# Mixture-of-experts stage of a two-layer transformer: scatters issued ahead of the gathers on GpSimd's queue

## What is computed

```python
x = x + _L0_attn_ref(_layernorm(x), w, w_out)             # linear attention, 16 heads
x = x + _L0_ffn_ref(_layernorm(x), router_w, w1, b1, w2, b2)   # the experts
x = x + _L1_attn_ref(_layernorm(x), w_attn, w_proj)       # causal attention, one key/value head
x = x + _L1_ffn_ref(_layernorm(x), wf_re, wf_im, bias)    # a filter in frequency space
```

## Time and profile before

| what | value |
|---|---|
| median of 3 runs | 752.31 us (749.36 to 752.98) |
| the profiled execution, its own time | 752.71 us |
| its span, first to last instruction | 751.0 us |
| TensorE busy | 618.1 us (82%), 4111 matmuls |
| VectorE busy | 521.4 us (69%) |
| ScalarE busy | 374.9 us (50%) |
| GpSimd busy | 391.2 us (52%) |
| 64 gathers (line 1045), POOL busy | 62.6 us, 978 ns each |
| 56 scatters (line 1036), POOL busy | 89.4 us, 1597 ns each |
| mean granted TensorE clock | 0.956 |

### The profile page before, as it was taken

How to read it: one execution, slowest core, us unless ns; L and a number is a source line. 1 busy time by engine, 2 the same in 40 slices (tenths; PEclk the granted TensorE clock), 3 DMA queues, 4 the chain that set the end, 5 groups by cost and what they waited for, 6 DMA issues and landing times.

```text
span 751.0 us, 14209 instructions
## 1 busy us (share of the span) xinstructions
PE 618.1 (82%) x4111; PEld 369.9 (49%) x4111; DVE 521.4 (69%) x1779; ACT 374.9 (50%) x800; POOL 391.2 (52%) x529
## 2 busy tenths in 40 slices
PE   2478888888405999999799778999999999999894
PEld 1235555554302688776566533545454545444453
DVE  8458888887794112225478859898989898987554
ACT  0322333331450423326622357777777777767873
POOL 0077777776004777776887554343434343433341
PEclk9989999999855999999999989999999999999997
DMA  9400000000040122244663244040304030200011
GB/s 297 133 0 1 1 0 0 0 1 0 16 140 28 49 43 39 39 93 84 110 98 35 26 82 53 10 59 10 59 10 60 9 60 9 60 5 2 24 52 42
DMA packets 45145, 34.55 MB, mean 46 GB/s; under 512 B 4304, under 2 KB 41728, under 8 KB 45072
## 3 DMA queue, kind: packets, MB, share of 16 engines
q1 hardware_dynamic: 33584, 25.15, 14.5%
q0 software_dynamic: 10144, 7.90, 7.5%
q10 hardware_dynamic: 1344, 0.62, 0.3%
HBM read 14.13 MB, written 9.70 MB: 32 GB/s over the span
## 4 chain that ended last, share of the span: by engine, by line
PE 46%; DVE 16%; issue 8%; ACT 4%; POOL 1%; DMA 1%; DVEq 0%; ACTq 0%; POOLq 0%
PE bank L2146 8%; PE wide L1275 6%; DVE masked L1744 6%; PE wide L2133 5%; PE wide L2082 5%; PE wide L1283 4%; PE bank L1283 4%; PE bank L2082 2%; PE wide L2158 2%; ACT L282 1%; DVE mx L1744 1%; DVE slot_t L886 1%; POOL x_row L1045 1%; PE bank L2057 1%; PE bank L1300 1%
## 5 line engine op out<-in xcount | busy, mean ns | idle before, releaser
L1941 ACT ACTIVATE pexp<-wide 128x512 f32<-128x512 f32 (+2 forms) x384 | 180.9, 536 | 77.9 <-PE wide L2133 75.9
L1744 DVE CUSTOM_DVE_ANT_0 masked<-wide,mask_qk 128x128 f32<-128x128 f32 (+3 forms) x423 | 182.8, 477 | 46.9 <-PE wide L2082 46.1
L1872 POOL TENSOR_SCALAR_AFFINE_SELECT pexp<-pexp 128x256 f32<-128x256 f32 x256 | 106.4, 429 | 166.7 <-ACT pexp L1941 165.2
L2133 PE MATMUL wide<-qT,kTe 128*128 128x256 bf16 (+3 forms) x512 | 121.8, 301 | 6.1 <-ACT pexp L1941 3.7
L2082 PE MATMUL wide<-kTm,qT 128*128 128x128 bf16 (+3 forms) x423 | 102.6, 300 | 13.2 <-DVE mx L1744 10.8
L1036 POOL DMA_INDIRECT x_dram<-yg,row_u x56 | 89.4, 1597 | 30.6 <-DVE yg L1088 15.7
L1225 ACT ACTIVATE hT<-wide,b1T 128x512 f32<-128x512 f32 x64 | 43.9, 686 | 100.7 <-PE wide L1275 100.7
L1045 POOL DMA_INDIRECT x_row<-xln_dram,row_u x64 | 62.6, 978 | 52.5 <-DVE slot_tok L915 33.6
L2146 PE MATMUL bank<-pexp,vx 128*32 128x512 f32 (+3 forms) x1024 | 85.4, 446 | 4.9 <-POOL pexp L1872 4.9
L2133 PEld LDWEIGHTS wide<-qT,kTe 128*128 128x128 bf16 x512 | 48.6, 99 | 42.5 <-ACT pexp L1941 23.1
L1275 PE MATMUL wide<-xgT,w_sb 128*128 128x512 f32 x128 | 67.4, 612 | 1.5 <-ACT xgT L1218 1.5
(11 more groups left out here) (282 smaller groups left out, 1046.6 us busy)
## 6 DMA issues: line engine op xcount, KB each, us to landing
qT<-qp SPq DMA_DIRECT2D x126, 64.0 KB
x_sb<-in_L_attn_x SPq DMA_DIRECT2D x8, 256.0 KB, 6.7
w_sb<-in_L_ffn_w SPq DMA_DIRECT2D x1, 2048.0 KB, 13.1
xln_dram<-hT SPq DMA_DIRECT2D x8, 256.0 KB, 2.3
x_dram<-x_sb SPq DMA_DIRECT2D x7, 256.0 KB, 2.7
x_sb<-x_dram SPq DMA_DIRECT2D x7, 256.0 KB, 3.1
out_x<-x_sb SPq DMA_DIRECT2D x7, 256.0 KB, 2.3
qT<-qp_first SPq DMA_DIRECT2D x18, 64.0 KB
```

The costliest lines, as they stand in the source:

```text
L1744: ins = nc.vector.tensor_tensor_reduce(out=masked[:, n % 4, at], in0=bank_of(n)[:, at], in1=mask_qk[:, T - w:T], scale=1.0, scalar=LEAST, ...
L1872: nc.gpsimd.affine_select(out=pexp[:, at, :, 0:P], in_=pexp[:, at, :, 0:P], pattern=[[0, 2], [1, P]], compare_op=ALU.is_ge, fill=0.0, base ...
L1941: nc.scalar.activation(pexp[:, exp_slot(b, 2 * step + h // 2), h % 2:h % 2 + nh, 0:w], scores_bank(b, m)[:, 0:nh * w].rearrange("p (h t) - ...
L2133: ins = nc.tensor.matmul(scores_bank(b, m)[:, hh * w:(hh + 1) * w], kTe[:, par, j * P:(j + 1) * P], qT[:, b % QB, 4 * qd + h + hh, j * P:T ...
```

## The change

In `moe_pool`, the gathers for the phase four further on are issued ahead of the wait for `m_y` in phases 0 to 3 only. In phases 4 to 11 they are issued behind that wait and behind the scatters of the phase, and ahead of the two small copies.

```diff
+        SCATTERS_LEAD = 4
+
         def moe_pool(pool):
...
             for p in range(PHASES):
-                if p + 4 < PHASES:
+                if p < SCATTERS_LEAD:
                     pool_moe_gathers(pool, p + 4)
                 pool.wait_ge(m_y, p + 1)
                 if p == E:
                     pool.wait_ge(m_xw[1], 16 * len(DMA_SECOND))
                 for b in half_of(p):
                     if b in BY_DMA:
                         pool_moe_scatter(pool, p % E, b)
+                if SCATTERS_LEAD <= p < PHASES - 4:
+                    pool_moe_gathers(pool, p + 4)
                 if p == E + 1:
                     pool_v(pool, 0, 0)
                 if p == E + 2:
```

## The result

The changed kernel takes 770.83 us (median; the kernel before, run beside it, 752.55). The ratio is 1.0251, with a 95% interval of 1.0216 to 1.0286: slower by some 18 us. One of its four executions took 3373.09 us, counts as a slow one and stands outside the ratio; the other three took 770.58 to 770.84. The same file, measured a second time further down, took 774.52 us, ratio 1.0277 (1.0255 to 1.0299).

The account below looks back on a forecast made before the run. TensorE, busy in all 44 us from 305 to 349 us, was taken as the bound, later POOL's round. Delays reaching 7.6, 13.7, 15.4 and 19.1 us on 752.7 made 771.8, less 0.4: 771.4 us, range 763 to 779.

Parts of the forecast that it names:

- Step 1: Transposes of phase 8: their gathers, now behind the scatters of phase 4, land late and stop TensorE for 4.6 us.
- Step 2: Behind the stop at phase 8: the granted clock falls, costing 3.0 us, so TensorE is 7.6 us late.
- Step 3: Transposes of phases 9 and 10: both gather blocks land in time, the second by 0.4 us, so no stop.
- Step 4: Transposes of phase 11: stop of 4.7 us, 1.6 beside another wait; clock falls again, 3.0; TensorE 13.7 us late.
- Step 5: Second half: POOL's round becomes the bound, with stops of 2.2 us at phase 13 and 4.3 at 15; TensorE 19.1 late.
- (b): Rival: it costs more, through slower landings beside the query rows or a third stop with its clock; 774 to 779, chance 0.12.
- The gain: Scatters no longer behind the next gathers: only the next scatter ever waited for one, 0.6 us in all; costed at nothing.
- The cost of a later S7: Scatters of phase 7: SP's loads of the first half's rows wait for them; said to move only as VectorE's output does.
- The signs: Marks expected in the trace, among them 15 to 20 us of gather waits and no POOL gaps over 2.5 us late on.
- (a): Rival: the clock doesn't fall behind the stops, 14.1 us late, 766.4; one fall of the two some 769; chance 0.20.
- (c): Rival: no difference, the gathers are in time all the same; 752.3 us, chance 0.03.
- (d): Rival: faster, as query rows land sooner and TensorE's 1.59 us stop ahead of the first maxima goes; 750.7, chance 0.03.

Follow-up runs that it names:

- the experiment with the wait alone: Against the kernel before: in phases 4 to 11 the gathers move behind the wait for VectorE's output but stay ahead of the scatters; 757.11 us, ratio 1.0055.
- The filled kernel: The changed kernel with 5, 5, 3 and 6 extra matmuls ahead of TensorE's wait for the gathers of phases 8, 11, 12 and 14; 770.22 us, ratio 1.0247.

## Why the prediction was right, point by point

The predicted 771.4 us stand against 770.83 and 774.52 measured, with a range of 763 to 779. The first agreement is closer than the working deserves, and that is luck: the stage was mis-sized by 2.5 and 3.4 us (19.1 for 21.6 and 22.5), and in the first measurement a front that was shorter by chance took that back. With the front of the kernel before, 752.3 and the measured stage make 774 to 775.

- **Step 1, right.** The stop at phase 8 is 4.53 us for a predicted 4.6. Alone, with its clock, it makes 6.6 us of the final time.
- **Step 2, right.** The clock's 3.0 us were 3.3 in the first profile and 4.2 in the second (y6 with and without the stop filled), and 2.7 with phase 4 alone. The mean over the 8 us behind the stop was 0.57, as predicted, and 0.50 in the second profile.
- **Step 3, right.** No stop at phases 9 and 10, and moving phase 6 alone costs nothing.
- **Step 4, right.** 4.56 us for 4.7, the clock at 0.63 over 8 us, and y9 late by 13.2 and 14.4 for 13.7.
- **Step 5, right in kind, wrong in its phases and too small.** "POOL's round becomes the bound" holds: with the rows held back the stage is still 21.8 us longer. But I followed the odd blocks, G13 (stop 2.2) and G15 (4.3), and the kernel stops at the even ones, G12 (3.16) and G14 (5.86). The sum had no landing for G12 and G14 at all, and for the block beside the query rows I took 3.0 us, while the last gather of G14 had 6.7 us to its reader. The transposes for phases 12 and 14 were in the trace before:

```profile
360.32 0.60 PE L1267 MATMUL wide<-cst,x_row 128*128 128x128 f32 x4
...
386.97 0.60 PE L1267 MATMUL wide<-cst,x_row 128*128 128x128 f32 x4
```

With the terms of step 5, S8 starts at 349.2 + 10.8 = 360.0, the last gather of G12 at 371.9, and with 2.5 us it lands at 374.4, wanted at 360.32 + 13.7 = 374.0. There was no slack, so any slower landing had to stop TensorE there. What I had in the rivals (b) as a risk on the last rounds was in the main line. The total was off by less, because a stop at phase 14 takes the place of the one at phase 15. With the query rows held back for both blocks the kernel comes near to what I wrote: a stop of 4.05 at phase 15, y12 late by 16.6 and y13 by 21.8 (15.4 and 19.1).
- **The gain, nothing, right as far as tested.** Where the order was changed and no gather came late (phase 6 alone), the time is that of the kernel before, and the scatters of the changed kernel still wait for one another for 0.6 us in all. The run with five buffers does not bear on this, since its queue is the old one.
- **The cost of a later S7.** The prediction said only that S7 moves as y7 does, which was true in the changed kernel. That a few us more would be paid in full was not seen; the experiment with the wait alone showed it, 5.7 us for 5.
- **The signs.** S12 starts 20.2 us later than before, counted from y4 (predicted 19). Two signs were missed a little: TensorE waits 22.8 us for gathers in all (21.0 in the second profile), not 15 to 20, and POOL has a gap of 2.69 us ahead of S10, not under 2.5.
- **Rivals.** (a), a clock that doesn't fall, is refuted by both profiles. The filled kernel, which keeps the clock up over the first two stops only, has 19.6 us in the stage and not the 14.1 of (a). (c) and (d) needed a lead of 12 us; phases 8 and 11 have 7.4 and 7.3, and both stopped.

What is not settled: why the second profile of the changed kernel is 0.8 us longer from y4 to y15 than the first, with the same stops within 0.8 us. Its clock was at 0.50 over the 8 us from 318.5 us, behind the first stop, where the first profile has 0.57; that fits, but no run isolates it. Nor does any run show what the new order does to the landings in the second half, where the query rows are under way as well.

## What to carry to other kernels

For each transfer in an engine's queue compare two times: from the moment that releases its issue, over all that stands ahead of it in the queue, to its landing; and from that same moment to the reader. Here the first was 12.0 us for 7.4 to 12.4 us of the second, and whether moving a block cost 6.6 us or nothing hung on that alone. Put what is read soonest first in the queue; a wait may stand ahead of it if the lead allows, a run of long issues may not. And write the queue out in full before comparing two loops: the one with its scatters first and its gathers five phases ahead looks like the change, but gives the old queue and the old time.

## What the runs showed of the hardware

The last gather of a block comes 4 to 5 us later beside 18 SyncE transfers of 64 KB than without them (6.7 us from issue to reader in the changed kernel, 7.8 us to landing with the rows held for phase 14, against 2.5), and holding these back moves the delay to the next block (a stop of 9.29 us) unless they are held past it. The issue alone is what fills POOL: 0.94 to 1.21 us for a gather of 128 rows and 1.54 to 1.88 for an adding scatter in the changed kernel, plus 0.3 us each. A stop of 4.5 us costs 2.7 to 4.2 us more through the clock. And an edit in the middle of the kernel has to be measured against a front that differs by 4.3 us from one execution to the next; a stretch within the profile (here y4 to y15, 123.2 us before the change, and within 0.6 us of that in the three experiments without a loss) is the finer measure.
